# Causal attention scores: three fp16 products of split operands in place of one fp32 product

## The reference, cut to what matters

```python
def _L3_attn_ref(x, Wq, Wk, Wv):
    q = jnp.einsum('btc,dc->btd', x, Wq)
    k = jnp.einsum('btc,dc->btd', x, Wk)
    v = jnp.einsum('btc,dc->btd', x, Wv)
    scale = 1.0 / jnp.sqrt(jnp.asarray(x.shape[-1], x.dtype))
    att = jnp.einsum('btd,bsd->bts', q, k) * scale
    causal = jnp.tril(jnp.ones((x.shape[1], x.shape[1]), dtype=bool))
    att = jnp.where(causal[None, :, :], att, -jnp.inf)
    w = jax.nn.softmax(att, axis=-1)
    return jnp.einsum('bts,bsd->btd', w, v)

t = t + _L3_attn_ref(_ln_t(t), L3_attn_Wq, L3_attn_Wk, L3_attn_Wv)
```

## Time and profile before

| | us |
|---|---|
| median of three runs | 7712.57 |
| lowest and highest | 7707.59, 7712.93 |
| span of the profiled execution | 7975.8 |
| TensorE busy in it | 7187.8 (90%) |
| VectorE, ScalarE, POOL busy in it | 5972.5, 4078.3, 3659.8 |

### The profile page before, as it was taken

One profiled execution on the slowest core, in us unless ns is written; L12 is line 12 of the kernel. 1 busy time (PEld: TensorE's weight loads), 2 busy tenths in 40 slices (PEclk: granted clock), 3 DMA queues, 4 the chain that ended last, 5 costly groups with the idle time before them and its releaser, 6 DMA issues. The chain is left out here.

```text
span 7975.8 us, 170513 instructions
## 1 busy us (share of the span) xinstructions
PE 7187.8 (90%) x62522; PEld 6186.6 (78%) x62522; DVE 5972.5 (75%) x9085; ACT 4078.3 (51%) x8541; POOL 3659.8 (46%) x4037
## 2 busy tenths in 40 slices
PE   8999899998999989999756788879988999999999
PEld 6888778886788867888546666645667989989999
DVE  7999889997899978999644555545556767767677
ACT  5888668885688757888311222224543222222222
POOL 5888658885688847888355555410000000000000
PEclk9999999999999999999878899889998999999999
DMA  2333223332233322333366555400003434434343
GB/s 66 90 93 93 75 64 92 93 90 68 74 90 93 92 58 83 90 94 90 109 174 171 164 160 152 119 4 3 0 6 95 125 116 125 125 116 128 113 129 108
DMA packets 590364, 763.42 MB, mean 96 GB/s; under 512 B 51703, under 2 KB 527896, under 8 KB 587585
## 3 DMA queue, kind: packets, MB, share of 16 engines
q1 hardware_dynamic: 537921, 585.72, 25.8%
q0 software_dynamic: 51840, 169.91, 7.5%
HBM read 721.77 MB, written 33.66 MB: 95 GB/s over the span
## 5 line engine op out<-in xcount | busy, mean ns | idle before, releaser
L647 POOL TENSOR_TENSOR l_arena<-l_arena 128x768 f32<-128x768 f32 x1536 | 2591.3, 1688 | 449.1 <-DVE l_arena L579 443.6
L579 DVE TENSOR_TENSOR_SCAN l_arena<-l_arena,psum 128x772 f32<-128x772 f32 x1536 | 2664.5, 1751 | 176.6 <-PE psum L406 72.5
L500 ACT ACTIVATE l_arena<-l_arena,l_A 128x384 f32<-128x384 f32 x3072 | 1643.7, 604 | 38.2 <-DVE l_arena L579 32.7
L408 PE MATMUL psum<-l_arena 128*128 128x128 f32 x11520 | 1499.3, 280 | 46.8 <-DVE l_arena L579 43.0
L408 PEld LDWEIGHTS psum<-l_arena 128*128 128x128 f32 x11520 | 1367.4, 192 | 170.5 <-issue 146.7
L419 PE MATMUL psum<-l_ident,l_arena 128*128 128x128 f32 x9216 | 1257.6, 273 | 50.6 <-ACT l_yT L506 41.7
L419 PEld LDWEIGHTS psum<-l_ident,l_arena 128*128 128x128 f32 x9216 | 1055.2, 141 | 60.2 <-POOL l_arena L647 60.2
L2269 POOL TENSOR_TENSOR st_mab<-st_xr 128x384 f32<-128x384 f32 x8 | 7.8, 1000 | 2053.1 <-DVE st_xr L2259 2053.1
L1211 POOL DMA_INDIRECT l_G<-neighbours,l_idx x648 | 621.2, 959 | 650.2 <-PE psum L1259 301.0
L490 ACT ACTIVATE l_arena<-l_arena,l_BT 128x256 f32<-128x256 f32 x1728 | 747.0, 496 | 7.5
L2544 ACT ACTIVATE st_own_s<-psum 128x384 f32<-128x384 f32 x256 | 125.7, 491 | 1092.5 <-PE psum L2381 1092.5
(11 more groups left out here) (436 smaller groups left out, 11291.5 us busy)
## 6 DMA issues: line engine op xcount, KB each, us to landing
l_arena<-c_rows SPq DMA_DIRECT2D x1536, 192.0 KB, 3.1
st_FS<-filter_sums SPq DMA_DIRECT2D x128, 1155.0 KB, 9.2
st_F<-filter_parts SPq DMA_DIRECT2D x128, 320.5 KB, 7.2
neighbours<-l_xt SPq DMA_DIRECT2D x256, 72.0 KB
st_mab<-in_st_mp SPq DMA_DIRECT2D x68, 256.0 KB, 9.5
st_mab<-in_st_mm SPq DMA_DIRECT2D x68, 256.0 KB, 6.2
l_G<-neighbours,l_idx POOLq DMA_INDIRECT x648
l_arena<-in_x SPq DMA_DIRECT2D x4, 1152.0 KB, 5.2
```

The lines of the kernel that those rows point to most:

```text
L408: mm = pe.matmul(ps[:, o:o + P], dtuT[:, g % 2, t, h * P:(h + 1) * P], diagB[:, rank[s] % 3, t, :], start=True, stop=True)
L500: act.activation(decay[:, s % NDC, half(h)], dtv[:, g % 2, h, :], ACT.Exp, scale=A[:, g // NRC, h, n:n + 1]).then_inc(s_exp, 1)
L579: dve.tensor_tensor_scan(hbuf[:, n, run], decay[:, s % NDC, run], x2_ps[s % 2][:, run], 0.0, ALU.mult, ALU.add).then_inc(s_scan, 1)
L647: pool.tensor_tensor(hC[:, s % NHC], halves(hbuf[:, s % NS, :]), Cs[:, s % NCS, :].unsqueeze(1).broadcast_to([P, 2, RC]), ALU.mult).then_i ...
```

## The change

q and k are no longer kept in fp32. Ahead of the loop the new first block takes the norms of the weights: VectorE squares `wq` and `wk` and sums along the rows, TensorE sums over the partitions with a product of two columns, ScalarE takes the inverse root (logarithm, exponential), and VectorE forms `grow` (a factor for q and one for k, so that they fit the range of fp16) and `shrink` (1/sqrt(C) over the product of the two factors). In the projection ScalarE writes the high part, fp16 of `grow` times the product, and VectorE, new there, the low part, fp16 of what is left over. TensorE now waits in chunks 4 to 15 for the low part of chunk n-4 (`s_pl`) in place of the copy. In `scores` each chunk is the sum of three fp16 products: high q with high k, high q with low k, low q with high k. The copy of the scores is scaled by `shrink`, an operand with one value per partition, in place of a constant.

```diff
-        q, k, v = sb("q", [P, L]), sb("k", [P, L]), sb("v", [P, TB, C])
+        v = sb("v", [P, TB, C])
+        qk = sb("qk", [P, 2, 2, L], F16)
...
+        s_pl, s_wq, s_wn, s_wl = (sem(n) for n in ("low_parts", "weights_squared", "norms_spread", "norms_raised"))
...
-            @block.gpsimd
-            def _(pool):
-                pool.wait_ge(s_w, 16 * len(loads))
+            @block.vector
+            def _(dve):
+                st = Steps(dve, s_wq)
+                dve.wait_ge(s_w, 16 * len(loads))
+                st.mark(dve.tensor_tensor(wsq[:, 0], wq[:], wq[:], ALU.mult))
+                st.link(dve.tensor_tensor(wsq[:, 1], wk[:], wk[:], ALU.mult))
+                st.mark(dve.tensor_reduce(wn[:], wsq[:], AX.X, ALU.add))
+                dve.wait_ge(s_wn, 1)
+                st.link(dve.tensor_scalar(wn[:], ps[:, 4 * BANK:4 * BANK + 2], 1e-20, None, ALU.max))
+                dve.wait_ge(s_wl, 2)
+                st.link(dve.tensor_scalar(grow[:], wn[:], TOP, None, ALU.mult))
+                st.link(dve.tensor_tensor(shrink[:], grow[:, 0:1], grow[:, 1:2], ALU.mult))
+                st.link(dve.reciprocal(shrink[:], shrink[:]))
+                st.mark(dve.tensor_scalar(shrink[:], shrink[:], scale, None, ALU.mult))
+
+            @block.tensor
+            def _(pe):
+                pe.wait_ge(s_wq, 3)
+                pe.matmul(ps[:, 4 * BANK:4 * BANK + 2], ones_c[:], wn[:], start=True, stop=True).then_inc(s_wn, 1)
+
+            @block.scalar
+            def _(act):
+                act.preload_act_table_set("natural_log_exp_and_others")
+                act.wait_ge(s_wq, 4)
+                act.activation(wn[:], wn[:], ACT.Ln).then_inc(s_wl, 1)
+                act.wait_ge(s_wl, 1)
+                act.activation(wn[:], wn[:], ACT.Exp, scale=-0.5).then_inc(s_wl, 1)
...
                 def _(dve):
                     dve.tensor_copy(xb[:], xn[:, ds(b * L, L)]).then_inc(s_xb, 1)
+                    for n in range(2 * NRC):
+                        i, c = n // NRC, n % NRC
+                        dve.wait_ge(s_pc, b * NPJ + n + 1)
+                        dve.scalar_tensor_tensor(qk[:, i, 1, c * RC:(c + 1) * RC], ps[:, BANK * (n % 4):BANK * (n % 4) + RC], grow[:, i:i + 1],
+                                                 qk[:, i, 0, c * RC:(c + 1) * RC], ALU.mult, ALU.subtract).then_inc(s_pl, 1)
...
-                        if n >= 4:
+                        if 4 <= n < 4 + 2 * NRC:
+                            pe.wait_ge(s_pl, b * 2 * NRC + n - 3)
+                        elif n >= 4:
                             pe.wait_ge(s_pc, b * NPJ + n - 3)
...
-                            act.activation((q, k)[n // NRC][:, c * RC:(c + 1) * RC], src, ACT.Copy).then_inc(s_pc, 1)
+                            i = n // NRC
+                            act.activation(qk[:, i, 0, c * RC:(c + 1) * RC], src, ACT.Copy, scale=grow[:, i:i + 1]).then_inc(s_pc, 1)
...
-                            pe.matmul(ps[:, BANK * (g % 2):BANK * (g % 2) + n], q[:, i * P:(i + 1) * P], k[:, o:o + n],
-                                      start=True, stop=True).then_inc(s_s, 1)
+                            for m, (qpart, kpart) in enumerate(((0, 0), (0, 1), (1, 0))):
+                                mm = pe.matmul(ps[:, BANK * (g % 2):BANK * (g % 2) + n], qk[:, 0, qpart, i * P:(i + 1) * P],
+                                               qk[:, 1, kpart, o:o + n], start=(m == 0), stop=(m == 2))
+                            mm.then_inc(s_s, 1)
...
                                 act.activation(S[:, i % 3, o:o + n], ps[:, BANK * (g % 2):BANK * (g % 2) + n], ACT.Copy,
-                                               scale=scale).then_inc(s_sc, 1)
+                                               scale=shrink[:, 0:1]).then_inc(s_sc, 1)
```

More of the change, by code:

```diff
@@ L1856, in layer3_attention @@
         ones_c, ident, mask = sb("ones_c", [P, P]), sb("ident", [P, P]), sb("mask", [P, P])
-        q, k, v = sb("q", [P, L]), sb("k", [P, L]), sb("v", [P, TB, C])
+        v = sb("v", [P, TB, C])
+        qk = sb("qk", [P, 2, 2, L], F16)
+        wsq, wn = sb("wsq", [P, 2, C]), sb("wn", [P, 2])
+        grow, shrink = sb("grow", [P, 2]), sb("shrink", [P, 1])
         S = sb("S", [P, 3, L])
@@ L1865, in layer3_attention @@
             "loaded", "x_copied", "projected", "proj_copied", "out_divided", "out_turned"))
+        s_pl, s_wq, s_wn, s_wl = (sem(n) for n in ("low_parts", "weights_squared", "norms_spread", "norms_raised"))
         s_s, s_sc, s_nm, s_e, s_v, s_t, s_tc, s_o, s_res, s_fr = (sem(n) for n in (
             "scores", "scores_copied", "row_max", "exp", "dve", "turned", "turned_copied", "out", "residual", "rows_free"))
+        scale = 1.0 / float(np.sqrt(np.float32(C)))
+        TOP = 2.0 ** 15 / P
         with nc.Block() as block:
@@ L1872, in _ @@
                     sp.dma_start(dst, src).then_inc(s_w, 16)
-            @block.gpsimd
-            def _(pool):
-                pool.wait_ge(s_w, 16 * len(loads))
+            @block.vector
[23 more added lines that the diff above has]
+                act.activation(wn[:], wn[:], ACT.Exp, scale=-0.5).then_inc(s_wl, 1)
         normalize(nc, ctx, sem, "ca_ln", ps, xres, xn, ones_c[:], w["eps5"])
         NPJ = 2 * NRC + TB // 3
-        scale = 1.0 / float(np.sqrt(np.float32(C)))
         with nc.Fori(0, NB) as b:
```

## The result

The changed kernel takes 7908.06 us (median of four runs, 7904.65 to 7909.76) against 7712.75 for the kernel before on the same chip: a ratio of 1.0258, with a 95% interval of 1.0243 to 1.0272. The forecast was 7695.1, in a range of 7686 to 7706. It is wrong in sign and far outside the range.

The account below looks back on a forecast made before the run. TensorE was taken to bound attention rows 6 and later. Four batches saving 5.3 each (-21.2), set-up +3.4 and semaphores +0.3 gave -17.5, so 7712.6 became 7695.1 us, range 7686 to 7706.

Parts of the forecast that it names:

- is a difference in the attention stage: Whole kernel: the attention stage's saving, -17.5 us, was set against the timed median of 7712.57.
- the list of what would make the prediction wrong: Attention: score passes further apart than 0.216, clock in 5484 to 5566 not 1.0, or a longer projection.
- the 0.08 for slower: Whole kernel: chance given to a time slower by more than the 0.2% line (15.4 us).
- the clock: Rival, score rows 8 to 17: longer bank pauses bring 1.2 GHz, time rises by 58 to 7770; chance 0.04.
- the weight loads: Rival, score blocks: fp16 loads not hidden, up to 0.1 per pass, +13 in all, 7726; chance 0.04.
- set-up, up to the first copy of xb: Ahead of the batches, once: serial chain forming the scale factors costs 3.4 us, bounds 2.5 and 5.
- rows 0 to 5: Early attention rows: savings not passed on in full; +0.2 us saved a batch, bounds -0.5 and +0.4.
- rows 6 to 17: Attention rows carried by TensorE: pass their score-block saving on in full, 5.1 us a batch.
- The score block: Attention scores: three fp16 passes of 0.216 make a 512-column chunk 0.65 instead of 0.86.
- The range's lower end: Whole kernel: 7686, the time given for the cheap bounds.
- the wait for a bank: Score blocks: from a chunk's end to the next chunk's start in the same bank, 0.97 instead of 0.95.
- the rule of the Trainium skill on cycled PSUM banks: Score blocks: 512-column bf16 products with cycled PSUM banks make the clock swing; cited for the clock rival, chance 0.04.

Follow-up runs that it names:

- the loop back at a resident start: Changed kernel with 35 unused one-column products (140 instructions) at the head of the last stage's TensorE program: 7680.49 us, ratio 0.9966 to the kernel before.
- its three padded forms: Kernel before with 112, 56 or 188 instructions of unused one-column products at the head of the last stage: 7935.48, 7852.05 and 7699.27 us.
- six runs of its padded forms: Changed kernel with 140 or 256 instructions of unused products ahead of the loop, some also with the score scale or low products edited: 7649.18 to 7912.59 us.

## Why the prediction was wrong

**The step that failed** stands in its first paragraph: that the sum "is a difference in the attention stage". The cost of every added instruction was taken as the time that its engine spends on it, and a stage without an edited line as one that keeps its time. The added TensorE instructions also take room in the program, and they moved a later loop from a start at which it stays resident to one at which it doesn't. That term, +222, was in no rival and at no bound, and the list of what would make the prediction wrong looked at the attention only; the 0.08 for slower rested on the clock and the weight loads. With the loop back at a resident start the change measures 7680.5 against 7706.8, 26 less, where 17.5 was forecast.

The trace of before held the hint, unread: 348 packets on the instruction queue, none of them in the loop that fills most of the last stage, so this loop of 6.5 blocks lived on staying resident. The Trainium skill ("Runtime: NRT & Kernel Launch", Instruction fetch mechanics) says that code is fetched in blocks of 256 instructions, that TensorE's memory for it holds 2,048, and that a taken branch to a block outside a window of two stalls until that block is fetched. The packets of 16,384 B, the period of 256 and the stall of 2.18 behind the jump agree. The window of two does not: by the count above, a loop over seven blocks ran without a packet. The same section of the Trainium skill also says that crossing a border is mostly hidden. Here seven of the nine packets of an iteration come without a stall of TensorE, but the border behind the jump costs 4.26. And 2,048 would be eight blocks, whereas here a loop that touches seven stays and one that touches eight, by the count above, does not. Nine packets for eight blocks would fit a queue that also fetches the block behind the loop's end; seven and one would then fill the eight. No run here tests it.

**The attention, term by term.** The trace of after, against the earlier trace rows of before, in us for all four batches (the stages differ by 24.1; the rest is rounding):

| part | predicted | measured |
|---|---|---|
| set-up, up to the first copy of xb | +3.4 | +3.2 |
| projections | 0 | +1.1 |
| rows 0 to 5 | -0.8 | +0.7 |
| rows 6 to 17 | -20.4 | -22.6 |
| last rows' transposes and outputs | 0 | -6.6 |
| semaphores | +0.3 | 0 |
| sum | -17.5 | -24.2 |

The score block was right. The range's lower end was not what its own bounds give (they add up to some 7689, not 7686), which changes nothing here. The timeline of the block of row 16 in the changed kernel (the rows of products are read through stretches that move on by one pass, so that each shows the start of the first of three):

```profile
5278.39 0.81 PE L1966 MATMUL psum<-ca_qk 128*128 128x512 f16 x3
...
5278.61 0.81 PE L1966 MATMUL psum<-ca_qk 128*128 128x512 f16 x3
...
5278.82 0.81 PE L1966 MATMUL psum<-ca_qk 128*128 128x512 f16 x3
...
5279.24 1.33 ACT L2031 ACTIVATE ca_S<-psum,ca_shrink 128x512 f32<-128x512 f32 x2 [2.86 <-PE psum L1966]
...
5280.84 1.34 ACT L2031 ACTIVATE ca_S<-psum,ca_shrink 128x512 f32<-128x512 f32 x2 [0.27 <-PE psum L1966]
```

The passes start 0.216 apart, as forecast. The third copy starts 1.60 after the first: 0.647 and 0.955, forecast 0.65 and 0.97. The copy takes 0.689 where 0.67 was taken. The nearest row gave 73 ns for the operand at 512 columns, the Trainium skill ("ScalarE: Activation LUTs", What ACT_TABLE_LOAD costs) 93, and 92 was measured: here the Trainium skill was right and the row, a bias operand of another line, was not. The handoffs around the copy were some 0.04 shorter, so the wait for a bank came out at 0.95 against 0.97 all the same. A row saved up to 0.1 more than its share, 0.5 a batch.

**The clock** went the other way from the rival. In the earlier trace rows the granted clock is 0.90 from 5566 to 5586. The table by stretch of before, finer, around TensorE's stall of 1.94:

```profile
5568.50:5570.00 1.50, 1.50 (x9) 1.50 (x9) 0.02 (x1) 0.47 (x3) 0.00 (x0) 0.50 0.00 0
5570.00:5572.00 2.00, 2.00 (x12) 2.00 (x12) 0.67 (x1) 0.00 (x0) 0.00 (x0) 0.54 0.00 0
```

And at the same place of after, the stall and the stretches around it:

```profile
5299.82 1.16 PE L1976 MATMUL psum<-ca_v,ca_PT 128*128 128x128 f32 x8 [1.59 <-DVE ca_PT L2073]
```

```profile
5299.00:5301.00 2.00, 1.18 (x10) 1.18 (x11) 1.35 (x3) 2.00 (x1) 0.00 (x0) 1.00 0.00 0
5301.00:5303.00 2.00, 2.00 (x20) 2.00 (x19) 0.91 (x2) 0.49 (x3) 0.00 (x0) 1.00 0.00 0
```

Before, TensorE stood 1.94 and then ran at 1.2 GHz until 5572; after, it stood 1.59 and stayed at 2.4 GHz. That is 6.3 of the 6.6 in the table: 0.35 to 0.4 from the shorter stall in each batch, and 1.6 of half clock in three of the four. The prediction priced a clock lost in the score blocks, and did not ask what the change would do to a stall that already cost clock. The shorter stall is not the work of the shorter blocks. VectorE's copies of row 16, which stand ahead of the stall, began behind an idle time of 0.36 on "issue" before, and without one after:

```profile
5566.92 1.29 DVE L2034 COPY ca_PT<-psum 128x512 f32<-128x512 f32 x2 [0.36 <-issue]
```

```profile
5299.08 1.29 DVE L2073 COPY ca_PT<-psum 128x512 f32<-128x512 f32 x2
```

Why it went (the change moves VectorE's program too) no run shows. So some 6 of the 24 us gained in the attention are luck. In the score blocks the clock held, with gaps of 0.30 in front of the third and fifth chunks:

```profile
5221.00:5297.00 76.00, 73.18 (x524) 55.14 (x522) 51.82 (x97) 46.84 (x79) 0.00 (x0) 1.00 0.01 1
```

So the rule of the Trainium skill on cycled PSUM banks ("TensorE: Matmul & The Clock Gate", A second HAM failure mode), which the prediction weighed, isn't borne out by this shape. The early rows did lose a little to the clock: in the first and the last batch rows 0 to 2 took 5.60 instead of 4.34, and the granted clock was 0.83 from 5211 to 5221 and from 5576 to 5586.

**The rest.** The projection's copies and low parts took what was forecast (0.58 and 0.61):

```profile
L1947 ACT ACTIVATE ca_qk<-psum,ca_grow 128x384 f16<-128x384 f32 x48 | 27.9, 581 | 34.7 <-PE psum L1932 32.6
...
L1918 DVE SCALAR_TENSOR_TENSOR ca_qk<-psum,ca_grow,ca_qk 128x384 f16<-128x384 f32 x48 | 29.6, 617 | 16.2 <-ACT ca_qk L1947 15.3
```

A projection became 0.1 to 0.6 longer, the 0.6 where its granted clock was 0.75; a longer projection was one of the prediction's own signs of being wrong. VectorE still idles 0.50 in front of row 4's first copy (0.3 or more was forecast), and the copies of xb, from which a batch is read, are 121.7 apart (forecast 123.2; before 128.5):

```profile
5222.66 0.69 DVE L2073 COPY ca_PT<-psum 128x512 f32<-128x512 f32 x1 [0.50 <-PE psum L1988]
```

```profile
L1914 DVE COPY ca_xb<-ca_xn x4: 1359/1360/1361, 5195.4 to 5560.5; 128x2304 f32 x4
```

## What to carry to other kernels

An edit that adds instructions to an engine moves every loop behind it in that engine's program. Before trusting a sum over the edited stage, look for later loops whose body is near what stays resident (here 1669 instructions, 6.5 blocks of 256) and that run without instruction packets: each is a rival whose price is its number of iterations times a fetch stall and the clock behind it. When a kernel comes out slower, compare it stage by stage first, and read "issue" in front of products together with the packets of the instruction queue; if they have grown, move the code by a hundred instructions before judging the change.

## What the runs showed of the hardware

- A TensorE loop of 1669 instructions ran at 55.4 us an iteration with no instruction packets at three of six starts, and at 60.3 to 66.1 with some nine packets of 16,384 B at the other three. Moving it by 256 instructions left its behaviour as it was.
- 112 instructions of no use, put where TensorE idles, cost 229 us in 7707; 140, put ahead of the changed kernel's loop, took it from a ratio of 1.0258 to 0.9966, some 225 us.
- In the attention, stalls of 1.91 to 1.96 before the last row were followed by half clock in 12 of 16 batches (the kernel before and its three padded forms); stalls of 1.58 or 1.59 in none of 28 (the changed kernel and six runs of its padded forms). The length alone does not decide it: in 4 of the 16 the clock held.
- A per-partition scale operand adds 92 ns to a ScalarE copy of 512 columns (597 to 689) and 87 to one of 128 (275 to 362).
